# A perceiver block on one core: one matmul for both parts of v, earlier output projections, later weight loads, earlier gate integers

## The reference

```
x = x + xattn(layernorm(x), ctx, lens)   # x (4,128,512), ctx (4,2048,512), 16 heads of 64
x = x + attn(layernorm(x))               # causal self-attention, 16 heads, biases
x = x + ffn(layernorm(x))                # 512 -> 1536 -> 512

xattn: qh, kh = rms_norm(q @ Wq), rms_norm(kv @ Wk); vh = kv @ Wv
       o = softmax(mask(qh kh^T / 8)) vh ; return o @ Wo
ffn:   x = act_qdq(x); up = act_qdq(x @ qdq4(w_up).T); gate = act_qdq(x @ qdq4(w_gate).T)
       gate = act_qdq(gate * fixed_u16(sigmoid(gate)))
       return act_qdq(gate * up) @ qdq4(w_down).T
act_qdq(x): scale = max|x| / 32767; clip(round(x / scale)) * scale   # one scale per tensor
```

## Time and profile before

| | |
|---|---|
| median of 3 runs | 1208.76 us (1208.14 to 1210.6) |
| the profiled execution's own time | 1208.0 us |
| its span, first to last instruction | 1205.6 us |
| TensorE busy | 1156.6 us, 96% |
| GpSimd, VectorE, ScalarE busy | 72%, 68%, 61% |
| mean granted TensorE clock | 0.994 |

### The profile page before, as it was taken

How to read it: one execution, slowest core, us unless ns; L and a number is a source line. 1 busy time by engine, 2 the same in 40 slices (tenths; PEclk the granted TensorE clock), 3 DMA queues, 4 the chain that set the end, 5 groups by cost and what they waited for, 6 DMA issues and landing times. The chain is left out here.

```text
span 1205.6 us, 31423 instructions
## 1 busy us (share of the span) xinstructions
PE 1156.6 (96%) x11864; PEld 879.6 (73%) x11864; DVE 818.9 (68%) x1798; ACT 737.3 (61%) x1332; POOL 869.7 (72%) x749
## 2 busy tenths in 40 slices
PE   7999999999999999899999999999998999889988
PEld 5777778877888888688888888888885677444433
DVE  6878777786766678677676788676765644542784
ACT  6367566775676667666676776766666436612751
POOL 4599899987989898788889888898897622510600
PEclk9999999999999999999999999999999999999999
DMA  7579999999999999999999998999999624975000
GB/s 229 143 135 194 210 179 202 204 222 193 184 216 192 206 186 231 201 192 209 191 191 206 218 223 167 217 185 204 196 190 237 180 88 71 183 190 83 1 1 35
DMA packets 560581, 210.50 MB, mean 175 GB/s; under 512 B 506800, under 2 KB 525232, under 8 KB 560432
## 3 DMA queue, kind: packets, MB, share of 16 engines
q1 hardware_dynamic: 538544, 168.64, 74.5%
q10 hardware_dynamic: 21888, 39.86, 11.8%
HBM read 66.79 MB, written 23.07 MB: 75 GB/s over the span
## 5 line engine op out<-in xcount | busy, mean ns | idle before, releaser
L147 PE MATMUL pair<-arena 128*128 128x256 f16 x2048 | 561.0, 274 | 12.3 <-DVE arena L672 8.2
L148 PE MATMUL pair<-arena 128*128 128x256 f16 x2048 | 559.9, 273 | 0.0
L149 PE MATMUL pair<-arena 128*128 128x256 f16 x2048 | 559.9, 273 | 0.0
L514 POOL TENSOR_TENSOR p_parts<-probs,p_parts 128x512 f16<-128x512 f32 x256 | 312.9, 1228 | 27.7 <-ACT p_parts L621 27.2
L524 POOL TENSOR_TENSOR k_rinv<-k_ms,half_neg 128x8 f32<-128x8 f32 x128 | 228.2, 1783 | 92.6 <-DVE k_ms L737 92.5
L147 PEld LDWEIGHTS pair<-arena 128*128 128x128 f16 x2048 | 200.5, 98 | 87.3 <-issue 51.9
L722 DVE CUSTOM_DVE_ANT_0 probs<-bank,mask 128x512 f32<-128x512 f32 x256 | 175.2, 685 | 126.0 <-PE bank L887 111.0
L621 ACT ACTIVATE p_parts<-probs 128x512 f16<-128x512 f32 x256 | 160.9, 629 | 117.8 <-DMA pt<-p_parts 106.7
L149 PEld LDWEIGHTS pair<-arena 128*128 128x128 f16 x2048 | 200.9, 98 | 24.1
L148 PEld LDWEIGHTS pair<-arena 128*128 128x128 f16 x2048 | 200.7, 98 | 21.2
L598 ACT ACTIVATE probs<-probs,neg_max 128x512 f32<-128x512 f32 x256 | 182.9, 715 | 10.0 <-DVE neg_max L731 9.9
(11 more groups left out here) (287 smaller groups left out, 1882.6 us busy)
## 6 DMA issues: line engine op xcount, KB each, us to landing
raws<-in_ctx_t_dram SPq DMA_DIRECT2D x58, 256.0 KB, 4.0
side_kept<-side_parts ACTq DMA_DIRECT2D x40, 256.0 KB, 4.5
arena<-side_kept SPq DMA_DIRECT2D x40, 256.0 KB, 4.8
w_kept<-ffn_turned ACTq DMA_DIRECT2D x36, 256.0 KB, 3.3
side_raw<-in_w_qkv_dram ACTq DMA_DIRECT2D x24, 256.0 KB, 3.3
arena<-w_kept SPq DMA_DIRECT2D x24, 256.0 KB, 3.7
pt<-p_parts SPq DMA_TRANSPOSE x240, 4.2
ffn_raw<-in_w_gate_dram ACTq DMA_DIRECT2D x12, 256.0 KB, 3.5
```

The costliest lines, as they stand in the source:

```text
L147: nc.tensor.matmul(to, x_hi[k], w_hi[k], start=(k == 0), stop=False)
L148: nc.tensor.matmul(to, x_hi[k], w_lo[k], start=False, stop=False)
L149: mm = nc.tensor.matmul(to, x_lo[k], w_hi[k], start=False, stop=(k == n - 1))
L514: nc.gpsimd.tensor_tensor(p_parts[n % PTS][:, 1, :], probs[n % PROBS][:, :], p_parts[n % PTS][:, 0, :], ALU.subtract).then_inc(p_lo_done, 1)
```

## The change

Five edits. (1) v's parts lie side by side in `v_both`; the high P moves both at once (130 columns) and the low P only v's high part (65), so a tile of keys takes two matmuls instead of three. The two sums lie in separate columns, bank 7 is cleared over 260 columns, and VectorE adds them up (`tensor_reduce` into `o_sum`); TensorE may clear the bank when this is done. (2) The output projections and norms of the drain stand one slot earlier, and wait only for the half of `wo` they read. The slot with the two useless matmuls is gone. (3) In self-attention one weight tile is loaded per part group, not two; the other eight follow the last `o_turned`. (4) Gate integers 2 to 5 are made before the up scale is known, and up tile 0 moves from VectorE to ScalarE. (5) `WARM_PRODUCT` is 3, not 4.

```diff
-OUT_FIRST, NORM_AT, WO_FIRST = (258, 262, 266), (262, 266), 249
+OUT_FIRST, NORM_AT, WO_FIRST = (257, 261, 265), (261, 265), 249
-WARM_DRAIN, WARM_PRODUCT = 2, 4
+WARM_DRAIN, WARM_PRODUCT = 2, 3
-        v_hi = [sb(f"v_hi{i}", [P, TILES, 2, VW], F16, c) for i in range(VS)]
-        v_lo = [sb(f"v_lo{i}", [P, TILES, 2, VW], F16, c) for i in range(VS)]
+        v_both = [sb(f"v_both{i}", [P, TILES, 2, 2, VW], F16, c) for i in range(VS)]
+        v_hi, v_lo = ([v[:, :, :, part, :] for v in v_both] for part in range(2))
-        o_new = bank[7][:, 0:2 * VW].rearrange("p (h v) -> p h v", h=2)
+        o_new = bank[7][:, 0:4 * VW].rearrange("p (h a v) -> p h a v", h=2, a=2)
@@ vector, a whole unit
-                    nc.vector.reciprocal(o_rec[u % 2][:, :], o_new[:, :, HD]).then_inc(rec_done, 1)
+                    nc.vector.tensor_reduce(o_sum[u % 2][:, :, :], o_new[:, :, :, :].rearrange("p h a v -> p h v a"), AX_X,
+                                            ALU.add).then_inc(sum_done, 1)
+                    dve.wait_ge(sum_done, u + 1)
+                    nc.vector.reciprocal(o_rec[u % 2][:, :], o_sum[u % 2][:, :, HD]).then_inc(rec_done, 1)
@@ tensor, values(slot)
-                        wait(pe, o_done, u)
-                        nc.tensor.matmul(bank[7][:, 0:2 * VW], zeros[:, 0:P], zeros[:, :], start=True, stop=False)
-                    to = o_new[:, h, :]
+                        wait(pe, sum_done, u)
+                        nc.tensor.matmul(bank[7][:, 0:4 * VW], zeros[:, 0:P], zeros[:, :], start=True, stop=False)
+                    to = o_new[:, h, :, :]
-                        nc.tensor.matmul(to, hi, v_hi[at % VS][:, t, h, :], start=False, stop=False)
-                        nc.tensor.matmul(to, hi, v_lo[at % VS][:, t, h, :], start=False, stop=False)
-                        mm = nc.tensor.matmul(to, lo, v_hi[at % VS][:, t, h, :], start=False,
+                        nc.tensor.matmul(to[:, 0, :], lo, v_hi[at % VS][:, t, h, :], start=False, stop=False)
+                        mm = nc.tensor.matmul(to, hi, v_both[at % VS][:, t, h, :, :], start=False,
@@ tensor, output projections of the drain
-                            pe.wait_ge(side_in[i], 64)
+                    if first % 4 == 0:
+                        pe.wait_ge(side_in[first // 4], 64)
@@ sync, self-attention
-                weights_turned(range(2 * n - 16, 2 * n - 14))
+                weights_turned([n - 8])
             o_turned(6)
             o_turned(7)
+            weights_turned(range(8, 16))
@@ feed forward
-    UP_ACT, UP_DVE, EARLY = (1, 2, 4, 5, 6, 8, 9, 10, 11), (0, 3, 7), 2
-    BARE = {k: i for i, k in enumerate(UP_ACT)}
+    UP_ACT, UP_DVE, EARLY, READY = (0, 1, 2, 4, 5, 6, 8, 9, 10, 11), (3, 7), 2, 6
+    BARE_TILES = UP_ACT[1:]
+    BARE = {k: i for i, k in enumerate(BARE_TILES)}
-            for k in range(EARLY, UP_ACT[0] + 1):
+            for k in range(EARLY, READY):
                 acted_int(k)
```

More of the change, by code:

```diff
@@ L194, in cross_attention @@
         mask = sb("mask", [P, CHUNKS, CHUNK], F32, c)
-        zeros = sb("zeros", [P, 2 * VW], F16, c)
+        zeros = sb("zeros", [P, 4 * VW], F16, c)
+        o_sum = [sb(f"o_sum{i}", [P, 2, VW], F32, c) for i in range(2)]
         lens_i = sb("lens_i", [P, B], I32, c)
@@ L245, in cross_attention @@
         s_done, s_max_done, head_max_done, neg_max_done = sems(c, "s_done s_max_done head_max_done neg_max_done")
-        p_done, p_hi_done, p_lo_done, pv_done, o_done = sems(c, "p_done p_hi_done p_lo_done pv_done o_done")
+        p_done, p_hi_done, p_lo_done, pv_done, sum_done, o_done = sems(c, "p_done p_hi_done p_lo_done pv_done o_sum_done o_done")
         pair, scores, q_bank = g["pair"], bank[4:6], bank[6]
-        o_new = bank[7][:, 0:2 * VW].rearrange("p (h v) -> p h v", h=2)
+        o_new = bank[7][:, 0:4 * VW].rearrange("p (h a v) -> p h a v", h=2, a=2)
         turned = [bank[i][:, :].bitcast(F16) for i in (6, 3)]
@@ L894, in _ @@
                     for i in range(WARM_DRAIN):
-                        nc.tensor.matmul(bank[0][:, :], ident16[:, :], v_hi[0][:, :, :, :].rearrange("p t h v -> p (t h v)")[:, 0:CHUNK],
+                        nc.tensor.matmul(bank[0][:, 0:4 * VW], ident16[:, :], v_both[0][:, 0, :, :, :].rearrange("p h a v -> p (h a v)"),
                                          start=True, stop=True)
@@ L940, in self_attention @@
         last_o, last_rec, last_parts = g["o_n"][1], g["o_rec"][1], g["o_parts"][1]
-        last_new = bank[7][:, 0:2 * VW].rearrange("p (h v) -> p h v", h=2)
+        last_new = bank[7][:, 0:4 * VW].rearrange("p (h a v) -> p h v a", h=2, a=2)
         NORMS = [("out", 2), ("out", 3)] + [("again", b) for b in range(B)]
@@ L1399, in divided @@
                                         rec[n % 2][:, :, :].unsqueeze(3).to_broadcast([P, 2, 4, HD]), ALU.mult).then_inc(o_done, 1)
[L1401 removed]
+            nc.vector.tensor_reduce(last_sum[:, :, :], last_new, AX_X, ALU.add).then_inc(last_sum_done, 1)
+            dve.wait_ge(last_sum_done, 1)
+            nc.vector.reciprocal(last_rec[:, :], last_sum[:, :, HD]).then_inc(last_rec_done, 1)
             dve.wait_ge(last_rec_done, 1)
[L1403 removed]
+            nc.vector.tensor_tensor(last_o[:, :, :], last_sum[:, :, 0:HD], last_rec[:, :].unsqueeze(2).to_broadcast([P, 2, HD]),
                                     ALU.mult).then_inc(last_o_done, 1)
@@ L1642, in _ @@
             for i, k in enumerate(UP_ACT):
-                nc.scalar.activation(up_i[:, k, :], up_raw[:, k, :], ACT.Abs, scale=raw_inv[:, UP:UP + 1]).then_inc(up_act, 1)
-                for after in range(max(k + 1, EARLY), UP_ACT[i + 1] + 1 if i + 1 < len(UP_ACT) else KF):
+                nc.scalar.activation(up_i[:, k, :], up_raw[:, k, :], ACT.Abs if k in BARE else ACT.Copy,
+                                     scale=raw_inv[:, UP:UP + 1]).then_inc(up_act, 1)
+                for after in range(max(k + 1, READY), UP_ACT[i + 1] + 1 if i + 1 < len(UP_ACT) else KF):
                     acted_int(after)
@@ L1756, in _ @@
             dve.wait_ge(tq_done, 2)
-            signs(UP_ACT[0])
-            top_of_all(PRODUCT, lambda: signed(UP_ACT[0]))
+            signs(BARE_TILES[0])
+            top_of_all(PRODUCT, lambda: signed(BARE_TILES[0]))
             scaled(PRODUCT, tq[:, 1:2])
@@ L1763, in _ @@
                 if k in BARE and BARE[k] + 1 < len(BARE):
-                    signs(UP_ACT[BARE[k] + 1])
-                    signed(UP_ACT[BARE[k] + 1])
+                    signs(BARE_TILES[BARE[k] + 1])
+                    signed(BARE_TILES[BARE[k] + 1])
                 dve.wait_ge(oi_done, k + 1)
```

8 lines of the change are left out of this document (4 added, 4 removed).

## The result

The changed kernel runs in 1193.88 us (median of 4, 1192.58 to 1195.68) against 1209.68 us for the kernel before (median of 4, 1208.14 to 1213.25): a ratio of 0.9888, with a 95% interval of 0.9859 to 0.9918. Six more runs in a later session gave 1190.04 against 1206.27, ratio 0.989 (0.9858 to 0.9922). It is faster, by 13.5 us by the ratio and 15.8 by the medians of so few runs. I forecast 1198, and 1193 to 1204 as the range: the time lies in it, 0.9 us inside its fast end, and the gain is 3 to 5 us more than the 10.4 of my sum.

A forecast was written before the change was run, and what follows sets the result against it. TensorE, busy for 96% of the span, was taken as the bound. Terms of -4.1 + 1.7 + 0.4 - 3.1 - 3.8 - 1.5 = -10.4 took 1208.0 to 1197.6; with 0.8 to the median, 1198 was forecast, range 1193 to 1204.

The forecast's parts named there:

- v's matmuls: Cross-attention: two matmuls per tile instead of three save 16 ns in each of 256 slots, 4.1 us less.
- Clearing: Cross-attention: clearing 260 columns of bank 7 instead of 130 costs 54 ns for each of 32 units, 1.7 us more.
- VectorE's extra work: Added reduction, 11.5 us of VectorE work, mostly hidden; 0.4 us more booked, at changes of batch (bounds 0 and 2.2).
- The drain: End of cross-attention: both pauses close and the useless matmuls go, 3.1 us less (bounds 1.5 and 3.6).
- The loads: Self-attention: fewer early weight loads bring part 13 in time and end a clock stretch, 3.8 us less (bounds 0 and 4.8).
- The feed forward: Products stretch: gate tiles run in ScalarE's idle time, so the maximum comes 1.5 us sooner (bounds 0.5 and 2).
- transfers keep the pace: Rival, cross-attention: DMA transfers set the pace and absorb the 4.1 us, giving 1202.5; chance 0.12.
- part 13 is late for another reason: Rival, self-attention: the loads don't delay part 13, or the clock's stretch falls elsewhere; 3.8 less gained, 1202.2; chance 0.15.
- the change does hardly anything: Rival, whole kernel: nothing from v's matmuls or the loads, half from the drain, 1207.9; chance 0.05.
- a clock stretch that goes away: Case faster than 1194, through a clock stretch that goes away at a block's border; chance 0.03.
- become the bound: Rival, cross-attention: VectorE's extra 0.36 us is exposed at every unit, so slower, 1213.6; chance 0.03.
- paced by its weight load: Rival, cross-attention: each 130-column matmul takes its neighbour's 97 ns weight load instead of 57, giving 1239; chance 0.02.

The follow-up runs named there:

- versions with three matmuls: The kernel before with the whole v edit, but still three 65-column matmuls per tile: 1207.25 us against 1206.27 for the kernel before, ratio 1.0012.
- the added one: The kernel before with the v edit alone plus one single-column matmul per tile: 1218.27 us against 1205.82 for the kernel before, ratio 1.0105.

## Why the prediction was right, and where its sizes were off

**v's matmuls** (-4.1). Shown: 14 to 17 ns a slot are 3.6 to 4.4 us. The rule that I set aside (the Trainium skill, TensorE: Matmul & The Clock Gate, section on the back-to-back issue gap) gives 81 ns in a stream of weight loads and matmuls of 128 columns; here 130 columns take 57 to 59 ns by the median, and the edit gained. But the reason that I gave, a fixed share of 3.8 ns that a matmul of any width pays, does not reach below 65 columns: there the spacing stays near 28 ns.

**Clearing** (+1.7). Shown: 0.11 us by its row and by the slots that lost it, and 2.1 +- 0.9 for clearing and sum together.

**VectorE's extra work** (+0.4). The instruction was sized right, the work was not: I took the quotient's length from the row of before, where one input was in PSUM, while the change moved it to SBUF. It cost 18 us of VectorE. By the rows above, the product ends when GpSimd's instruction does, and with the sum in PSUM all 31 products take 290 to 292 ns. The Trainium skill (SBUF — State Buffer, section on the two separate sides) has the rule: a VectorE instruction with two inputs in SBUF and a GpSimd instruction that reads SBUF exclude each other, and the later one waits for the whole of the other. The runs agree, 872 ns on average with both inputs in SBUF against 291 with one in PSUM. TensorE's waits for `k_n` in cross-attention (40 to 905 us) rose from 0.8 to 1.7 us in the five profiled executions without the v edit to 2.2 to 4.0 in seven with it. Not all of that is VectorE's extra work: the versions with three matmuls and with the added one have this work too, but slower slots, and waited 1.7 and 0.0 us. With the product short again (two executions) it is 2.2, against 3.1 to 4.0 in the five others of the seven. So the long product costs about 1 us, more than the 0.4 booked; that the rest comes of TensorE arriving sooner fits these numbers, but is not shown.

**What the v edit gave beyond my sum.** This term was mis-sized: -2.0 booked, -7.0 and -8.1 measured. The clock accounts for 2.3 of it (7.8 us lost before, 5.4 with the edit), and at full clock the edit is worth 4.2 +- 0.7 and 5.1 +- 1.0 in its two sessions, for 2.0. The waits for transposed probabilities were 1.5 to 7.6 us in the five without and 1.2 to 4.4 in the seven with the merged matmul. In three of the five the clock fell before the drain, each time in or right behind a standstill of 2.1 to 3.1 us, in one pause or two close together; the seven have no pause over 1.8 us there and no stretch at 1.2 GHz. But two pauses of 2.2 and 2.3 us in the kernel before had no fall behind them, two of the five had no stretch either, and neither had the versions with three matmuls and with the added one, so part of this is chance. The version with three matmuls has 13.9 us of waits between 40 and 905 us, the seven 7.7 to 11.8, the five 8.9 to 14.0, and the version with the added matmul 5.8. These ranges overlap; why two matmuls for three should shorten waits for a DMA stays open.

**The drain** (-3.1). The mechanism was right, both halves of `wo` are in time and the pause is gone. By stages it is worth 1.5 us at full clock (41.4 on average over seven profiled executions without, 39.9 over seven with), since a new wait on the score chunk took its place; that was the lower bound I named. Six of the seven without the edit also had a stretch at 1.2 GHz there, 3.4 or 6.8 us long, none with it. That I had not booked. Alone the edit gives nothing that can be measured, and in its trace self-attention takes 0.7 to 1.8 us more than in the six others with the old order of loads, with 1.4 us of waiting for a transpose that SP issues and a pause of 2.2 us ahead of an output projection. With the loads moved this is gone.

**The loads** (-3.8). Shown: 2.2 us at full clock (standard error 0.7) against 2.3, and about 1 for the clock against 1.5. The clock's part is chance per execution: the stretch at 1055 of the earlier trace rows was in one other of six profiled executions with the old order, and two of seven with the new order had one 2 to 3 us behind the end of the stage. What I forecast for the place came out: no pause at part 13, one of 0.9 us left ahead of the last output projection, SP done with its sixteen loads (8.01 us, 0.50 each) 3 us ahead of the block's end.

**The feed forward** (-1.5). 1.4 by the stage, 11.07 for 12.52 us by the rows.

**The sum.** In the later session the changed kernel is 9.6 us faster at full clock (standard error 1.2) and my terms without the clock add up to 8.9. The step that was off is the clock. I booked one stretch of 1.5 us at one place, read from one profiled execution; in that session the kernel before loses 8.1 us to it and the changed one 3.4, that is 4.7 us. Over all runs with a clock on record (67 and 10) it is 7.9 and 4.4, 3.5 us. In the profiled execution of the kernel before, 5.1 us of it lie ahead of the feed forward; in the two of the changed kernel 1.7 and 0. How much each closed pause bought is not shown. That 8.9 came so near owes something to two errors of opposite sign, too little for v and too much for the drain.

**The rivals.** That transfers keep the pace, that part 13 is late for another reason and that the change does hardly anything fell with v alone, the loads alone and the total. The 1193.88 lies just in the band below 1194 to which I gave 0.03, "through a clock stretch that goes away"; since the clock did give more than I booked, that chance was far too low. VectorE did not become the bound, though it is named for `k_n` where I had said it must not be. A wide matmul is not paced by its weight load of 97 ns: the starts lie 57 to 59 ns apart.

## What to carry to other kernels

Price a closed pause twice: its length, and half of the stretch at 1.2 GHz that follows it in some executions; take the second from the mean clock of many runs, not from the one trace, and leave out the stretches that fall where TensorE has no useful work. When an operand moves from PSUM to SBUF, the instruction's old duration is no longer its row: look whether both inputs are now in SBUF while GpSimd works. And before crediting a stage with a few microseconds, compare executions of kernels that don't differ in it.

## What the runs showed of the hardware

A matmul with its own weight load of 128 columns kept the stream for about 28 ns, whether it has 1 column (27.8) or 65 (29.5); 130 take 57 to 59, 256 take 109. A VectorE product over 128 elements took 291 ns with an input in PSUM and up to 1284 ns with both in SBUF, ending 0.15 us after GpSimd's instruction. The first matmul of a unit can start the accumulation for the whole bank, so that the other head's columns need no clearing of their own, as the two versions without the clearing matmul do it. And the mean granted clock of the same kernel, the one before, lay between 0.989 and 0.999 over the 67 runs of the experiments, its time between 1198 and 1212 us, with a correlation of -0.5 to -0.65 between the two.
